# Second half of each pair loaded over all partitions, six x buffers, pairs 0 and 1 turned by TensorE, loads ordered anew, last pair in two sets of banks

## The reference, cut to what matters

```python
xn = (x - mean(x)) / sqrt(var(x) + 1e-5)
s  = einsum('btd,dm->btm', xn, Win) + bin_          # 512 -> 64
h  = relu(s[..., None] * W1 + b1)                   # 64 channels, 16 hidden values each
g  = einsum('btmh,mh->btm', h, W2) + b2
ffn = einsum('btm,md->btd', g, Wout) + bout         # 64 -> 512
out = x + attention(xn) + ffn
# attention: q, k, v by Wq, Wk, Wv (512x512); three rounds on the first 16 tokens of a batch
# with 32x32 maps, layer norms and a softmax; then Wo and bo. Tokens past 16 get bo alone.
```

## Time and profile before

| | us |
|---|---|
| median of three runs | 378.41 |
| profiled execution | 379.16 |
| its span | 377.4 |
| busy: PE, DVE, ACT, POOL | 312.2, 280.2, 219.6, 237.7 |
| 16 DMA engines, queue of SP | 78.0% of the span |
| HBM read and written | 55.87 MB and 33.69 MB |

### The profile page before, as it was taken

How to read it: one execution, slowest core, us unless ns; L and a number is a source line. 1 busy time by engine, 2 the same in 40 slices (tenths; PEclk the granted TensorE clock), 3 DMA queues, 4 the chain that set the end, 5 groups by cost and what they waited for, 6 DMA issues and landing times.

```text
span 377.4 us, 5029 instructions
## 1 busy us (share of the span) xinstructions
PE 312.2 (83%) x1772; PEld 145.4 (39%) x1772; DVE 280.2 (74%) x426; ACT 219.6 (58%) x270; POOL 237.7 (63%) x209
## 2 busy tenths in 40 slices
PE   2576279979979999999799999989779794997952
PEld 1334054445424634453344443424243342432310
DVE  0759955689899899979999899769549583855332
ACT  2112357555757765757677688877538671787500
POOL 8336960582973969397684968978571949179500
PEclk9996779999989999999999999999969997999875
DMA  8999939798457898869488797969699997723634
GB/s 215 256 304 368 224 123 213 265 283 231 164 245 194 318 212 320 224 233 302 135 329 206 280 263 236 266 231 267 189 307 226 303 244 254 304 111 159 190 145 188
DMA packets 53512, 89.89 MB, mean 238 GB/s; under 512 B 5720, under 2 KB 38640, under 8 KB 49392
## 3 DMA queue, kind: packets, MB, share of 16 engines
q1 hardware_dynamic: 52640, 89.16, 78.0%
q0 software_dynamic: 640, 0.16, 0.6%
q10 hardware_dynamic: 208, 0.26, 0.3%
HBM read 55.87 MB, written 33.69 MB: 237 GB/s over the span
## 4 chain that ended last, share of the span: by engine, by line
PE 41%; DVE 26%; DMA 22%; issue 5%; SPq 3%; ACT 1%; POOL 1%; DVEq 0%; POOLq 0%
PE op L499 13%; DMA out_dram<-x 12%; DVE x L869 7%; PE s L445 7%; PE g L482 6%; DMA x<-in_L_attn_x_dram 5%; DVE stats L896 5%; DMA xq<-in_L_attn_x_dram 4%; PE T L432 4%; DVE xqT L879 3%; PE rep L466 3%; PE op L326 2%; DVE w2s L745 2%; DVE WvT L821 2%; DVE SL L890 1%
## 5 line engine op out<-in xcount | busy, mean ns | idle before, releaser
L1003 POOL TENSOR_TENSOR x<-x,bias_row 128x512 f32<-128x512 f32 x128 | 163.5, 1316 | 7.3 <-DVE bias_row L736 7.3
L627 ACT ACTIVATE H<-rep,b1c,w1c 128x1024 f32<-128x1024 f32 x128 | 146.5, 1215 | 31.0 <-PE rep L466 19.2
L869 DVE TENSOR_TENSOR x<-x,op 128x1024 f32<-128x1024 f32 x64 | 77.5, 1211 | 40.2 <-PE op L499 37.2
L896 DVE BATCH_NORM_STATS2 stats<-x 128x6 f32<-128x512 f32 x128 | 80.5, 678 | 23.0 <-DMA x<-in_L_attn_x_dram 23.0
L499 PE MATMUL op<-wout,G 64*128 64x512 f32 x256 | 83.8, 733 | 9.4 <-DVE x L869 9.3
L987 POOL TENSOR_TENSOR rstd<-veps,nhalf 128x8 f32<-128x8 f32 x16 | 26.3, 1647 | 87.6 <-DVE veps L906 87.5
L602 ACT ACTIVATE xT<-T 128x512 f32<-128x512 f32 x64 | 38.4, 600 | 65.4 <-PE T L432 65.1
L432 PE MATMUL T<-ident,x 128*128 128x128 f32 x256 | 45.5, 305 | 23.4 <-DMA x<-in_L_attn_x_dram 20.1
L482 PE MATMUL g<-H,w2s 128*32 128x512 f32 x512 | 63.7, 607 | 0.0
L445 PE MATMUL s<-xT,win 128*64 128x512 f32 x128 | 60.5, 617 | 3.6 <-DVE xqT L879 3.6
L445 PE MATMUL s<-xqT,winq 128*64 128x512 f32 x128 | 60.5, 617 | 0.0
(11 more groups left out here) (160 smaller groups left out, 268.2 us busy)
## 6 DMA issues: line engine op xcount, KB each, us to landing
x<-in_L_attn_x_dram SPq DMA_DIRECT2D x32, 1024.0 KB, 7.0
out_dram<-x SPq DMA_DIRECT2D x32, 1024.0 KB, 5.2
xq<-in_L_attn_x_dram SPq DMA_DIRECT2D x64, 256.0 KB, 8.2
x<-in_L_attn_Wq_dram SPq DMA_DIRECT2D x1, 1024.0 KB, 10.2
x<-in_L_attn_Wk_dram SPq DMA_DIRECT2D x1, 1024.0 KB, 13.2
x<-in_L_attn_Wv_dram SPq DMA_DIRECT2D x1, 1024.0 KB, 5.0
x<-in_L_attn_Wo_dram SPq DMA_DIRECT2D x1, 1024.0 KB, 5.5
bias_row<-in_L_ffn_bout_dram SPq DMA_DIRECT2D x1, 256.0 KB, 10.5
```

The source lines that it names most:

```text
L627: act.activation(Hr[half][k % len(Hr[half])][:, :], rep_ps[:, :], ACT.Relu, bias=b1c[:, half, k:k + 1], scale=w1c[:, half, k:k + 1]).then_ ...
L869: dve.tensor_tensor(both, both, o_ps[:, :].rearrange("p (h d) -> p h d", h=2), ALU.add).then_inc(add_done, 1)
L896: dve.bn_stats(stats[:, j, :], x_sb[m][:, j * D:(j + 1) * D]).then_inc(bn_done, 1)
L1003: pool.tensor_tensor(x_sb[m][:, c], x_sb[m][:, c], bias_row[:, :], ALU.add).then_inc(xc_done, 1)
```

## The change

- **Quads.** Per half pair, eight DMAs of 64 KB take the place of two of 256 KB: one for each 32-token block t, and each fills all 128 partitions with one run of 512 bytes. Source: 4 blocks of features (i) x 32 tokens (a) x 512 bytes. Destination: 128 rows x 512 bytes. Three buffers of half a pair instead of two of a whole one.
- **Pairs 0 and 1** have no quads: TensorE turns their second half too (eight groups in place of four, alternately in `T_ps` and `A_ps`), ScalarE copies it into `xT1`, over `xqT`.
- **Ring.** Six x buffers; load of pair n+2 in body n, behind the first store, in place of pair n+1 ahead of it.
- **Start.** Win ahead of x; pairs 0 and 1, rows, Wq, Wk, pair 2, its quads, Wv and Wo (now in the buffer of pair 5, without a wait), Wout and the small ones. `winq` goes to ScalarE's DMA queue. GpSimd issues its parameter DMAs ahead of its masks. Attention steps of bodies 0 to 2 get other places.
- **End.** The last pair's projections use `o_ps` and `rep_ps` in turn, and its stores go out tile by tile (512 KB).
- Small buffers are laid over others to make room.

```diff
-RING = 5
+RING = 6
+AHEAD = 2
+    QH = BLK // QD // 2
-        xq = [sb(f"xq{r}", [P, BLK // QD * P]) for r in range(2)]
+        xq = [sb(f"xq{r}", [P, QH * P]) for r in range(3)]
+        xT1 = xqT[:, :, :, :].rearrange("p t c a -> p (t c a)").rearrange("p (c n) -> p c n", c=DC)
+        BY_PE = 2
-        def load_quads(n):
-            if n > 1:
-                sp.wait_ge(tq_done, 2 * (n - 1))
-            for i in range(DC):
-                sp.dma_start(xq[n % 2][i * QD:(i + 1) * QD, :].rearrange("p (t d) -> p t d", d=P), xq_v[n, 1, i, :, :, :]).then_inc(ldq[n % 2], 16)
+        def load_quads(k):
+            r, n, h = k % 3, k // 2 + BY_PE, k % 2
+            if k > 2:
+                sp.wait_ge(tq_done, k - 2)
+            for t in range(QH):
+                sp.dma_start(xq[r][:, t * P:(t + 1) * P], xq_v[n, 1, :, :, h * QH + t, :]).then_inc(ldq[r], 16)
...
+            if n < N - 1:
...
+            else:
+                for j in (2 * i, 2 * i + 1):
+                    sp.wait_ge(add_done, TILES * n + j + 1)
+                    sp.dma_start(out_v[n, :, :, j * D:(j + 1) * D], by_tile(x_sb[m][:, :], j)).then_inc(st[m][i], 16)
         def sp_program():
...
+            load(sp, 0, 0)
+            load(sp, 0, 1)
+            load(sp, 1, 0)
+            load(sp, 1, 1)
...
             load_weight(0, Wq)
             load_weight(1, Wk)
+            load(sp, 2, 0)
+            load(sp, 2, 1)
+            load_quads(0)
+            load_quads(1)
+            load_weight(2, Wv)
+            load_weight(3, Wo)
...
+            load(sp, 3, 0)
+            load(sp, 3, 1)
+            load_quads(2)
+            load(sp, 4, 0)
+            load(sp, 4, 1)
+            load(sp, 5, 0)
+            load(sp, 5, 1)
+            for n in range(2, BODIES):
+                if n > 2 and has(n + 1):
+                    load_quads(2 * (n + 1 - BY_PE))
                 if has(n - 3):
                     store(n - 3, 0)
+                if n + AHEAD >= RING and has(n + AHEAD):
+                    for h in range(2):
+                        load(sp, n + AHEAD, h)
+                if has(n + 1):
+                    load_quads(2 * (n + 1 - BY_PE) + 1)
                 if has(n - 3):
                     store(n - 3, 1)
+        def bank(n, g):
+            return A_ps if n < BY_PE and g % 2 else T_ps
+        def sum_banks(n, j):
+            return rep_ps if n == N - 1 and j % 2 else o_ps
         def project(n, j):
...
-            if TILES * n + j > 0:
-                pe.wait_ge(add_done, TILES * n + j)
+            free = TILES * n + j - (1 if n == N - 1 and j > 0 else 0)
+            if free > 0:
+                pe.wait_ge(add_done, free)
         def turn_quads(n, h):
-            half = BLK // QD * P // 2
-            c = slice(h * half, (h + 1) * half)
+            if n < BY_PE:
+                return
+            k = 2 * (n - BY_PE) + h
+            dve.wait_ge(ldq[k % 3], 16 * QH * (k // 3 + 1))
             if h == 0:
-                dve.wait_ge(ldq[n % 2], 16 * DC * (n // 2 + 1))
-                if n > 0:
-                    dve.wait_ge(sc_done, DC * n)
+                dve.wait_ge(sc_done, DC * n)
```

More of the change, by code:

```diff
@@ L97, in residual_block @@
         row1 = Hr[0][0][:, 0:D]
-        w_nat = [x_sb[3][:, (i % 2) * DC * D:(i % 2 + 1) * DC * D].rearrange("p (c i) -> p c i", c=DC) for i in range(4)]
+        w_nat = [x_sb[3 + i // 2 * 2][:, (i % 2) * DC * D:(i % 2 + 1) * DC * D].rearrange("p (c i) -> p c i", c=DC) for i in range(4)]
         w_t = [t.rearrange("p (c o) -> p c o", c=DC) for t in
                (x_sb[4][:, 0:DC * D], x_sb[4][:, DC * D:2 * DC * D], sb("WvT", [P, DC * D])[:, :], sb("WoT", [P, DC * D])[:, :])]
-        small = sb("small", [HD, 3 * HD + NV])
         bqc, bvc, bqs = (sb(n, [P, DC]) for n in ("bqc", "bvc", "bqs"))
@@ L131, in residual_block @@
         qk = sb("qk", [P, 2, CR])
+        tile4, small = qk[0:HD, 0, 0:P], qk[0:HD, 1, 0:3 * HD + NV]
         over_v = flat(w_t[2])
@@ L149, in residual_block @@
         ld = [[sem(f"ld{r}{h}") for h in range(2)] for r in range(RING)]
-        ldq = [sem(f"ldq{r}") for r in range(2)]
+        ldq = [sem(f"ldq{r}") for r in range(3)]
         st = [[sem(f"st{r}{h}") for h in range(2)] for r in range(RING)]
@@ L158, in residual_block @@
         op_done, xc_done, add_done = sem("op_done"), sem("xc_done"), sem("add_done")
-        (in_xa, in_lna, in_win, in_wo2, in_rows, in_small, in_bq, in_scal, in_ffn) = (
-            sem(f"in_{n}") for n in ("xa", "lna", "win", "wo2", "rows", "small", "bq", "scal", "ffn"))
+        (in_xa, in_lna, in_win, in_winq, in_wo2, in_rows, in_small, in_bq, in_scal, in_ffn) = (
+            sem(f"in_{n}") for n in ("xa", "lna", "win", "winq", "wo2", "rows", "small", "bq", "scal", "ffn"))
         in_w = [sem(f"in_w{n}") for n in "qkvo"]
@@ L305, in pe_attention @@
             pe.wait_ge(ident_made, 2)
[L306 removed]
+            pe.wait_ge(in_win, 16)
             for c in range(DC):
@@ L311, in pe_attention @@
             pe.wait_ge(xn_made, 1)
+            pe.wait_ge(ev_done, groups(BY_PE))
             for c in range(DC):
@@ L421, in pe_attention, with groups, transpose @@
             mm.then_inc(att_ps, 1)
-        def transpose(n, c):
-            m = n % RING
[L426 to L433, removed]
+        def groups(n):
+            return DC * n + DC * min(n, BY_PE)
+        def bank(n, g):
+            return A_ps if n < BY_PE and g % 2 else T_ps
+        def transpose(n, part):
+            m = n % RING
+            for g in (2 * part, 2 * part + 1) if n < BY_PE else (part,):
+                b, c = divmod(g, DC)
+                if c == 0:
+                    pe.wait_ge(ld[m][b], 16 * (n // RING + 1))
+                free = groups(n) + g - (1 if n < BY_PE else 0)
+                if free > 0:
+                    pe.wait_ge(ev_done, free)
+                for j in range(TILES):
+                    col0 = b * HALF + j * D + c * P
+                    mm = pe.transpose(bank(n, g)[:, j::TILES], x_sb[m][:, col0:col0 + P], ident[:, :])
+                mm.then_inc(tr_done, 1)
         def s_product(n):
@@ L439, in s_product @@
                 pe.wait_ge(s_done, n)
-            pe.wait_ge(ev_done, DC * (n + 1))
-            pe.wait_ge(tq_done, 2 * (n + 1))
+            pe.wait_ge(ev_done, groups(n + 1))
+            if n >= BY_PE:
+                pe.wait_ge(tq_done, 2 * (n + 1 - BY_PE))
+            if n == BY_PE:
+                pe.wait_ge(win_centred, 2)
             for c in range(DC):
                 for b in range(2):
-                    w, turned_x = (win, xT[:, c, :]) if b == 0 else (winq, xqT[:, :, c, :])
+                    if b == 0:
+                        w, turned_x = win, xT[:, c, :]
+                    elif n < BY_PE:
+                        w, turned_x = win, xT1[:, c, :]
+                    else:
+                        w, turned_x = winq, xqT[:, :, c, :]
                     mm = pe.matmul(s_ps[b * M:(b + 1) * M, :], w[:, c, :], turned_x, start=(c == 0), stop=(c == DC - 1))
@@ L596, in act_attention, with evacuate @@
             act.activation(att, A_ps[:, 0:D // 2], ACT.Copy).then_inc(att_made, 1)
-        def evacuate(n, c):
-            act.wait_ge(tr_done, DC * n + c + 1)
-            if n > 0:
-                act.wait_ge(sc_done, DC * (n - 1) + c + 1)
-            act.activation(xT[:, c, :], T_ps[:, :], ACT.Copy).then_inc(ev_done, 1)
+        def evacuate(n, part):
+            for g in (2 * part, 2 * part + 1) if n < BY_PE else (part,):
+                b, c = divmod(g, DC)
+                act.wait_ge(tr_done, groups(n) + g + 1)
+                if n > 0:
+                    act.wait_ge(sc_done, DC * (n - 1) + c + 1)
+                act.activation((xT if b == 0 else xT1)[:, c, :], bank(n, g)[:, :], ACT.Copy).then_inc(ev_done, 1)
         def copy_rstd(n):
@@ L639, in act_program @@
             act.dma_start(lna, lna_w.partition_broadcast(RW)).then_inc(in_lna, 16)
+            for i in range(DC):
+                act.dma_start(winq[i * QD:(i + 1) * QD, :, :], Win.rearrange("(i j b) m -> i b j m", i=DC, b=QD)[i, :, :, :]).then_inc(in_winq, 16)
             side = [-PLACES, act_attention()]
@@ L746, in dve_attention @@
             ins.then_inc(w2s_made, 1)
+            yield next(AT_DVE)
+            dve.wait_ge(in_winq, 16 * DC)
+            dve.tensor_tensor(winq[:, :, :], winq[:, :, :], wmean[:, :].unsqueeze(1).to_broadcast([P, DC, M]), ALU.subtract).then_inc(win_centred, 1)
             for u in range(0, 4 * DC, 2):
@@ L909, in dve_program @@
             side = [-PLACES, dve_attention()]
-            reach(side, -1, 0)
             statistics(0, 0)
             statistics(0, 1)
+            reach(side, -1, 0)
             for n in range(BODIES):
@@ L999, in add_bias @@
                     pool.wait_ge(bias_made, 1)
-                pool.wait_ge(tr_done, DC * (n + 1))
+                pool.wait_ge(tr_done, groups(n + 1))
                 pool.wait_ge(var_done, n + 1)
```

(10 more changed lines are left out.)

67 lines of the change are left out of this document (21 added, 46 removed), and 6 rows, old and new, of the table AT_DVE.

## The result

The changed kernel takes 387.21 us (median of 4 runs), the kernel before 379.19 on the same chip: a ratio of 1.019, with a 95% interval of 1.012 to 1.026. The whole interval lies above 1, so it is slower, by 8 us and not by the 27 that were forecast; whether the loss passes 2% stays open. The page of the profiled execution (386.97 us, span 385.2): busy time, DMA by slice, SP's queue, and the chain that ended last by engine and by line.

A forecast was written before the change was run, and what follows sets the result against it. Four DMA engines carrying all quads were to bound the kernel, 24.3 us per body: 352 us of work (quads 196, x 81.0, stores 59.8) put the last quads at 359; with 45.3 and 1.8 more, 406 us (338 to 430).

The forecast's parts named there:

- The reading of the earlier trace: A GpSimd-queue DMA of the same form seemed to put data on four engines only; the new quads were expected to do likewise.
- signs named: For four engines: DMA share well under 78%, quads near 75 GB/s, xqT waits, s products 24 us apart, SP held 0.9 us.
- 512 x 27.4 ns = 14.0 us: Time each of four engines needs for one pair's quads: 512 runs at 27.4 ns each.
- four-engine case: Likeliest case, quads on the same four DMA engines throughout: 406 us, own range 398 to 430, chance 0.60.
- the sum: Work of the four engines up to the last quads: 352 us, with 196 for quads; last quads land at 359.
- No bubble: SP's program would leave the four engines no gap, each queue wait being met about half a body before.
- 2 + 3: Idle time allowed before the last quads: start 2 us, and 3 us while the weights are turned.
- Also over the 22.8 between two s products beside the attention: Four engines' 24.3 us per body was said to exceed the s products' 22.8 us spacing beside the attention too.
- End: Last four adds: two sets of banks let projections and adds overlap, saving 6.5 us, or 4 at the lower clock.
- Even-spread rival: Quads use all 16 engines, TensorE's 15.6 us bounds late bodies: 21, 12 and 6.5 us less, 340 us; chance 0.33.
- Ring of six: Takes the store wait off the late bodies' chain: up to 5.3 us each, 21 us; nothing if DMA engines lack room.
- SP's issues: Sixteen quad issues per pair at 0.4 us, 6.4 us, run beside the transfers and cost less than SP's earlier holding.

The follow-up runs named there:

- e1: The changed kernel with each half pair of quads loaded by four DMAs of 32 partitions, on 16 engines again: 342.72 us, ratio 0.904.
- e6: The changed kernel with each quad DMA cut in two by features (source 2 blocks x 32 tokens, destination 64 rows): 555.57 us.
- e4: The changed kernel with the last pair's projections all in the same two banks, each waiting for the add before: 393.11 us, ratio 1.036.
- e2: e1 with its quad DMAs cut in two, eight of 64 KB per half pair: 342.07 us, ratio 0.902.
- e5: e1 with the load of pair n+1 in body n, only after both stores of pair n-4, as with five buffers: 343.69 us, ratio 0.900.
- e10: The kernel before with one line moved, the quads of pair n+2 behind the second store: 361.03 us, ratio 0.952.

## Why the prediction was right or wrong

- **Direction and mechanism: right.** The reading of the earlier trace rows held on SP's queue: four semaphore writes per quad DMA, 28.8% of the engines' time in use, and e1 undoes it. Of the signs named, the lower DMA share, VectorE's waits for xq (38.8 us, though only nine waits) and SP held are there (1.2 us per quad issue in a late body, not 0.9); late s products are 21.3 to 23.5 us apart (the last two 16.2) and not 24, the rate 86 GB/s and not 75. One thing that was said of packets does not hold on GpSimd's queue: the destination of W1 has runs of 16 bytes, and its packets in the earlier trace rows are of 512, so a packet there holds many runs. The reading of four engines came out right all the same.
- **The step that failed: "512 x 27.4 ns = 14.0 us".** The record of a run lasts 27 ns, but the next one starts before it ends: 4 x 512 bytes at 86 GB/s are 23.8 ns per run, and e6 gives 2 x 512 / 43 = 23.8 again. I had divided the 5.56 us of records in the earlier trace rows by the runs, though 16 engines have only 4.8 us in a stretch of 0.3 us: with these it would have been (4.8 - 0.63) / 180 = 23 ns. Over 14 x 512 runs it is 14 x 512 x 3.6 = 26 us too much. The rate of a stretch is the price, not the length of a record. I had also set 27.4 as the lower bound, so the range of the four-engine case, 398 to 430, could not hold the result either.
- **What is left of the sum.** With the right price the last quads would have been there at 333 us; VectorE waited for them until 342.65. "No bubble" was nearly right: SP waited 38.5 us for adds ahead of stores with quads behind them, but counted from the packet records its queue has fewer than four packets in flight for only 5.7 us up to there, where 2 + 3 had been put down. So the missing 10 us are mostly not idle time. They may be the price of loads and stores, which the sum took at their best rates; no run tests that. From there to the end it took 42.6 us, not 45.3: 406 - 26 + 10 - 3 = 387.
- **"Also over the 22.8 between two s products beside the attention": this did not show.** Up to pair 8 the bodies hardly stretched (table of e1), though at the right price they hold 12.2 + 10.3 = 22.5 us of work for the four engines. The queue being so rarely short of packets, this suggests that it fell behind there and that the wait came due after the attention; it is not shown.
- **End: right.** 6.5 us forecast, 6.6 in the adds, 5.9 by e4.
- **Even-spread rival: right in size.** 340 was worked out for it, and e1 and e2 took 342.7 and 342.1. It was given 0.33; it would have decided if the runs had been spread. Its 21 us in the late bodies were 19.3, its 12 at the start 8.7 by pair 8, its 6.5 at the end 8.7 behind the last s product.
- **Ring of six: right sum, wrong cause.** I put the 5.3 us per late body on the buffer that waits for its store. e5 has that wait and not the loss, and the ring of six waits for the same stores. e10 shows that the store was late because of the quads ahead of it; that the sum came out was luck.
- **SP's issues: right.** 16 per pair cost nothing that e2 can show.
- **Where e1's 10% comes from.** By the table of e1, 8.7 us of 36.7 are gained up to pair 8, 19.3 between pairs 8 and 15, and 8.7 behind the last s product. In e10 the order of the queue alone takes those seven bodies from 128.6 to 110.5 us, nearly all of the middle part, and e4 shows 6 us of the last. The start was not tried alone.

## What to carry to other kernels

Before a DMA is reshaped to reach more partitions, see what both of its sides count outermost: a source of 4 blocks put every byte on the same four engines and took 44 us, more than the rest of a good change gave. Price a transfer by the rate of a stretch that holds it alone, and expect a slow transfer to show only where nothing else is slower: beside the attention it cost 2 us. And what stands between two stores in an in-order queue is paid by the load that waits for the second: one line moved gave 18.5 us.

## What the runs showed of the hardware that I had not expected

- The records of runs on one DMA engine overlap: 27 ns each, one every 23.8 ns, the same with four engines and with two.
- Engines in one DMA on SP's queue: four for 4 source blocks, two for 2, and the same ones again in the DMAs that follow (43 GB/s in e6).
- The granted clock of TensorE was 1.00 in e1's late stretches, where TensorE is never idle, and 0.85 on average in those of the changed kernel, where it is idle for 5 of 23 us, so that part of a body's lengthening comes back as slower matmuls (one of the projection, line 537: median 816 ns against 590).
